# Where TensorE's expert products stand against its spreading products: two places of a gated-expert kernel moved

## The chip, the cores and the metric

The kernel runs on one core of one Trainium2 chip. The metric is the device time of one execution in microseconds (us). Five engines work side by side and meet at semaphores: TensorE (PE), VectorE (DVE), ScalarE (ACT), GpSimd (POOL) and SyncE (SP), which only issues DMAs. Each engine takes its own instructions strictly in the order in which the program lists them, so an instruction that waits holds up all that stand behind it on its engine.

## What is computed

The input is x, 16 images of 64 channels and 112 x 112 positions, in float32.

```python
def _L0_conv_ref(x, conv_w, conv_b):
    pooled = jnp.stack([jnp.max(x, axis=1), jnp.mean(x, axis=1)], axis=1)
    y = conv 3x3 (pooled, 2 channels -> 1) + conv_b
    return x * sigmoid(y)

def _L0_ffn_ref(x, router_w, router_b, expert_w, expert_b):   # E = 8 experts, K = 2
    router_probs = softmax(x @ router_w + router_b)
    top_p, top_i = top_k(router_probs, K);  top_p = top_p / sum(top_p)
    expert_out = einsum('bnd,edc->bnec', x, expert_w) + expert_b
    return einsum('bnk,bnkc->bnc', top_p, take(expert_out, top_i))

x = x + _L0_conv_ref(_ln_c(x), conv_w, conv_b)        # norm over channels
t = tokens(x)                                         # one token per position, 64 values
t = t + _L0_ffn_ref(_ln_t(t), router_w, router_b, expert_w, expert_b)
```

So each position gets a scale from a small convolution, a router picks two of eight 64 x 64 experts for it, and the output is the input plus the two gated expert products.

## The kernel before, in words

The 16 images are 8 pairs; a pair fills the 128 partitions. A pair is worked in 14 steps of 8 image rows (896 columns, `TOK`, two halves of 448, `HALF`). Three stages run on different pairs at the same time, one round behind the other:

- **Centring (A)**, rounds 0 to 7: PE multiplies a transposed slice of the input by the centring matrix and the router weights (`centre_rows`, L493), two groups per step; ACT copies the result out (L942, L946) and squares it, DVE takes maxima and sums (L687, L697).
- **Gates (B)**, rounds 1 to 8: on whole-pair statistics. DVE works at fixed places between its other work: an inverse square root, then the top-two router (`gate`: L729 to L835). POOL has router products as well (L1240 to L1311). In step 2 PE makes the small convolution (L592, `convolve`), ACT its sigmoid (L1026, "sig").
- **Experts (C)**, rounds 2 to 10: step `v` of the pair two rounds back. PE turns the gates (`turn`, L507), ACT brings them to SBUF (L991), PE spreads them over partitions into PSUM (`spread`, L514), DVE multiplies spread gates by the input (`scale_unit`, L710, units 0 to 5), for units of POOL ACT first copies the spread gates out of PSUM ("gs", `gate_to_sbuf`, L999) and POOL multiplies (L1201), and PE multiplies the eight products by the expert weights (`experts`, L568). PE also spreads the scale of the convolution (`spread_a1`, L553), ACT copies it ("a1s", L1006), POOL multiplies it with the input ("tt", L1218), and DVE adds both (`finish`, L723). SP loads and stores.

Rounds 2 to 7 have all three stages ("rounds with centring"). Round 8 has gates and experts, round 9 experts alone, and round 10 is a short rest ("rounds without centring").

The spread gates have two PSUM slots. Slot 0 takes DVE's units 1, 2, 4, 5; slot 1 takes DVE's units 0 and 3 and both units of POOL, whose copy by ACT must be done before the slot is written again. So a spreading product of unit 2, 4 or 5 waits for the DVE unit before it in the slot (`scaled_d`). The order on PE in one step, with the names that the texts use:

- S1, SP1: spreading for DVE's unit 1 and POOL's second unit; E5': expert product of unit 5 of the step before; T: the turn for the next step; bias and E0
- S2, S3: the second spreading batch; centring group 0; E1, EP0 (unit 1 and POOL's first)
- S4, SP0': the third batch, for unit 4 and POOL's first unit of the next step; in step 2 of a round the convolution; E2; A1 (`spread_a1`); bias and E3
- S5, S0': the fourth batch, unit 5 and unit 0 of the next step; centring group 1; E4, EP1

Every E is two products of 448 columns, which the trace shows as four records (float32 takes two each). The waits: E2 waits for DVE's unit 2, as S4 does; E5' waits for unit 5 of the step before, as S1 does. SP0' waits for unit 3, SP1 for unit 0. `centre_rows` of group 1 waits for ACT's a1s copy, since both use the PSUM tile tm. In step 2 A1 waits for the sigmoid, for the same reason. ACT's order is gs for POOL's first unit, (in step 2 the sigmoid), a1s, squares, copy of centring group 1, squares. POOL takes its unit as soon as gs is copied and DVE has passed a given place of the gates, and then the tt product. DVE's order in a step: early gates, unit 1, finish, units 2 and 3, (maximum of group 0), late gates, unit 4, finish, unit 5, unit 0 of the next step, (maximum of group 1).

Of the kernel before, what the change touches and what calls it, by code (L numbers as in the profile page):

```python
# [135 lines left out]
def gated_expert_program(nc, x, conv_w, conv_b, router_w, router_b, expert_w, expert_b, const_f, const_g, out):  # L136
# [3 lines left out]
    with ExitStack() as ctx:  # L140
# [132 lines left out]
        def due(count):  # L273

            return count > 0
# [10 lines left out]
        def c_at(r, per_step, v, n):  # L286
            return at(r, 2, per_step * STEPS, per_step * v + n)
# [4 lines left out]
        def on(r, v):  # L292

            return 0 <= (r - 2) * STEPS + v < PAIRS * STEPS
# [173 lines left out]
        def _(pe):  # L468
# [5 lines left out]
            def centre_rows(r, step, g):  # L474
                if g == 0:
                    if due(count := at(r, 0, STEPS // XA * 16, (step // XA + 1) * 16)):
                        pe.wait_ge(ld_xa[step % XA], count)
                read_out(pe, r, step, g + 1 - len(centre_pairs(r)))
                v = step - LAG
                if on(r, v + 1) and g == 0:  # L480
                    if due(count := c_at(r, 1, v + 1, 1)):
                        pe.wait_ge(s_ready, count)
                if on(r, v + 1) and g == 1:
                    if due(count := c_at(r, 1, v + 1, 1)):
                        pe.wait_ge(a1_out, count)
                if step == 2 and g == 1 and r >= 2:
                    b_done(pe, r, B_ACT, "sig")
                pair = centre_pair(r, step, g)
                for j in range(GRP):
                    row = g * GRP + j  # L490
                    for b in range(2):
                        chans = slice(b * CH, (b + 1) * CH)
                        last = pe.matmul(pair[:, b, j, :],  # L493
                                         xa[chans, step % XA, row * W:(row + 1) * W], rhs1[chans, :],
                                         start=True, stop=True)
                last.then_inc(centred, 1)

            def turn(r, step, v):

                if due(count := c_at(r, 1, v, 1)):  # L500
                    pe.wait_ge(rest1, count)
                read_out(pe, r, step, 0)
                if due(count := c_at(r, 1, v - 1, 1)):
                    pe.wait_ge(a1_out, count)
                for j in range(ROWS):
                    for b in range(2):
                        last = pe.transpose(turn_out[b * SB:(b + 1) * SB, j * W:(j + 1) * W],  # L507
                                            parts[:, v % 2, j, b * SB:(b + 1) * SB], ident)
                last.then_inc(turned, 1)

            def spread(v, k, c, slot):
                for b in range(2):
                    rows = slice(b * SB + slot * QUAD, b * SB + (slot + 1) * QUAD)
                    last = pe.matmul(gb[:, 2 * slot + b, 0:HALF], cg[rows, k * P:(k + 1) * P],  # L514
                                     s[rows, v % 2, c * HALF:(c + 1) * HALF], start=True, stop=True)
                return last

            def spread_for_dve(r, v, i):

                if i == 0:  # L520
                    if due(count := c_at(r, NP, v, 1)):
                        pe.wait_ge(gate_out, count)
                elif i == 3:
                    if due(count := c_at(r, NP, v, 2)):
                        pe.wait_ge(gate_out, count)
                else:
                    before = {1: 0, 2: 2, 4: 3, 5: 5}[i]
                    if due(count := c_at(r, ND, v, before)):
                        pe.wait_ge(scaled_d, count)
                spread(v, D_PAIR[i], i // 3, 1 if i in (0, 3) else 0).then_inc(spread_d, 1)  # L530

            def spread_for_pool(r, v, j):

                if j == 0:
                    if due(count := c_at(r, 1, v, 1)):
                        pe.wait_ge(s_ready, count)
                    if due(count := c_at(r, ND, v - 1, 4)):
                        pe.wait_ge(scaled_d, count)
                else:
                    if due(count := c_at(r, ND, v, 1)):  # L540
                        pe.wait_ge(scaled_d, count)
                spread(v, P_PAIR, j, 1).then_inc(spread_p, 1)
# [15 lines left out]
            def biases(r, v, c):  # L558
                if due(count := c_at(r, 2, v - 1, c + 1)):
                    pe.wait_ge(final, count)  # L560
                for b in range(2):
                    pe.matmul(moe[b * CH:(b + 1) * CH, c, 0:HALF], bw[:, b * CH:(b + 1) * CH],  # L562
                              s[:, v % 2, c * HALF:(c + 1) * HALF],
                              start=True, stop=False, skip_group_check=True)

            def experts(u, k, c):
                for b in range(2):
                    last = pe.matmul(moe[b * CH:(b + 1) * CH, c, 0:HALF], wc[:, k * CH:(k + 1) * CH],  # L568
                                     gx[:, u, b, :], start=False, stop=(k == KT - 1), skip_group_check=True)
                last.then_inc(mixed, 1)  # L570

            def experts_of_dve(r, v, i):
                if due(count := c_at(r, ND, v, i + 1)):
                    pe.wait_ge(scaled_d, count)
                experts(i, D_PAIR[i], i // 3)

            def experts_of_pool(r, v, j):
                if due(count := c_at(r, NP, v, j + 1)):
                    pe.wait_ge(scaled_p, count)
                experts(ND + j, P_PAIR, j)  # L580
# [29 lines left out]
            def body(r, A, Bp, steps=STEPS):  # L610
                for step in range(steps):
                    v = step - LAG
                    cur, ahead = on(r, v), on(r, v + 1)

                    if cur:
                        spread_for_dve(r, v, 1)
                        spread_for_pool(r, v, 1)
                    if on(r, v - 1):
                        experts_of_dve(r, v - 1, 5)
                    if ahead:  # L620
                        turn(r, step, v + 1)
                    if cur:
                        biases(r, v, 0)
                        experts_of_dve(r, v, 0)

                    if cur:
                        spread_for_dve(r, v, 2)
                        spread_for_dve(r, v, 3)
                    if A:
                        centre_rows(r, step, 0)  # L630
                    if cur:
                        experts_of_dve(r, v, 1)
                        experts_of_pool(r, v, 0)

                    if cur:
                        spread_for_dve(r, v, 4)
                    if ahead:
                        spread_for_pool(r, v + 1, 0)
                    if Bp and step == 2:
                        convolve(r, A)  # L640
                    if cur:
                        experts_of_dve(r, v, 2)
                    if ahead:
                        spread_a1(r, step, v + 1, A, Bp)
                    if cur:
                        biases(r, v, 1)
                        experts_of_dve(r, v, 3)

                    if cur:
                        spread_for_dve(r, v, 5)  # L650
                    if ahead:
                        spread_for_dve(r, v + 1, 0)
                    if A:
                        centre_rows(r, step, 1)
                    if cur:
                        experts_of_dve(r, v, 4)
                        experts_of_pool(r, v, 1)

            early_body(0, False)
            early_body(1, True)  # L660
            pe.wait_ge(setup_dve, 2)
            body(2, True, True)
            for r in range(3, PAIRS):
                body(r, True, True)
            body(PAIRS, False, True)
            body(PAIRS + 1, False, False)
            body(PAIRS + 2, False, False, LAG + 1)
# [736 lines left out]
```

## Time and profile before

| | us |
|---|---|
| median of 3 runs (1415.57 to 1417.33) | 1415.97 |
| profiled execution | 1416.11 |
| span of its instructions | 1414.3 |
| PE busy | 1308.1 (92%) |
| DVE busy | 1240.0 (88%) |
| POOL busy | 1066.4 (75%) |
| ACT busy | 1053.7 (75%) |

The span is what the timeline covers, from 0 to 1414.3; 1.8 us of the profiled execution lie around it. PE and DVE are both near full, so a share over the whole span does not say which of them sets the end; that changes from step to step and has to be read in the timeline. A row of a timeline gives the start, the length of the merged records, engine, line, operation, tiles and count, and in brackets the idle time before and what ended it. Ends overlap a little with the next start, so distances are taken from start to start.

### The profile page before, as it was taken

The numbers are of one execution on the slowest core, as the hardware profiler recorded it, in microseconds if no ns is written. First come the engines' busy times: TensorE is split into PE (matmuls) and PEld (weight loads), VectorE is DVE, ScalarE is ACT, GpSimd is POOL, SyncE is SP. The second block draws the span as 40 slices with busy tenths as digits, with TensorE's granted clock in tenths as the row PEclk, the third lists the DMA queues.
The fourth block names the chain that finished last, engine by engine and source line by source line (L and its number), as shares of the span: only waits on it lengthen the run. The fifth ranks groups of instructions, "written<-read, shape, count | busy, mean of one in ns | idle before, by whom it ended". The sixth has DMA issues, their size and how long they took to land.

```text
span 1414.3 us, 33104 instructions
## 1 busy us (share of the span) xinstructions
PE 1308.1 (92%) x11750; PEld 617.7 (44%) x11750; DVE 1240.0 (88%) x1527; ACT 1053.7 (75%) x3950; POOL 1066.4 (75%) x643
## 2 busy tenths in 40 slices
PE   8864999999999999999999999999999898899998
PEld 8853444444444444444444444444444332233332
DVE  6787799979999899988999899988999789987776
ACT  5677789888988898888988889888898344444442
POOL 6333687887788787887888787887878887887765
PEclk9955899999999999999999999999999999999999
DMA  6442466667667666576666666676665555565663
GB/s 224 131 128 66 144 196 199 202 188 210 202 188 218 189 208 209 173 233 196 197 184 209 197 199 205 176 224 196 202 210 165 155 164 156 159 183 180 178 188 118
DMA packets 85845, 259.97 MB, mean 184 GB/s; under 512 B 13744, under 2 KB 13744, under 8 KB 85680
## 3 DMA queue, kind: packets, MB, share of 16 engines
q1 hardware_dynamic: 85680, 257.85, 60.5%
q8 instruction: 94, 1.54, 0.5%
q14 instruction: 71, 0.58, 0.1%
HBM read 206.42 MB, written 51.38 MB: 182 GB/s over the span
## 4 chain that ended last, share of the span: by engine, by line
PE 52%; DVE 24%; issue 12%; POOL 2%; ACT 1%; DVEq 0%; POOLq 0%; ACTq 0%
PE moe L568 30%; DVE gx L710 15%; PE gb L514 8%; PE tm L493 8%; DVE ge L732 2%; PE tm L507 2%; DVE stats L687 2%; PE moe L562 2%; DVE ot L723 1%; PE tm L553 1%; DVE oh L745 1%; PE tm L592 1%; DVE u L795 1%; POOL dl L1261 1%; DVE top L729 0%
## 5 line engine op out<-in xcount | busy, mean ns | idle before, releaser
L568 PE MATMUL moe<-gx,wc 128*64 128x448 f32 x3584 | 812.6, 553 | 0.0
L710 DVE TENSOR_TENSOR gx<-gb,xd 128x896 f32<-128x896 f32 x672 | 707.5, 1085 | 84.9 <-PE gb L514 84.4
L1201 POOL TENSOR_TENSOR gx<-gs,xd 128x896 f32<-128x896 f32 x224 | 492.9, 2201 | 249.7 <-ACT gs L999 181.6
L999 ACT ACTIVATE gs<-gb 128x896 f32<-128x896 f32 x224 | 205.2, 916 | 190.1 <-PE gb L514 184.6
L961 ACT ACTIVATE sq<-xct 112x64 f32<-112x64 f32 x1400 | 338.4, 246 | 7.5 <-DVE early_s L697 2.1
L568 PEld LDWEIGHTS moe<-gx,wc 128*64 128x64 f32 x3584 | 218.0, 136 | 193.5 <-issue 160.8
L961 ACT ACTIVATION_READ_ACCUMULATOR sq<-xct 112x1 f32 x1400 | 265.5, 190 | 0.0
L514 PE MATMUL gb<-s,cg 32*128 32x448 f16 x1792 | 187.1, 359 | 61.4 <-DVE gx L710 60.3
L1218 POOL TENSOR_TENSOR tt<-xc,a1s 128x896 f32<-128x896 f32 x112 | 235.0, 2098 | 11.3 <-issue 9.7
L514 PEld LDWEIGHTS gb<-s,cg 32*128 32x128 f16 x1792 | 51.5, 91 | 399.8 <-DVE gx L710 333.7
L493 PE MATMUL tm<-rhs,xa 64*112 64x74 f32 x2800 | 185.5, 274 | 10.5 <-ACT early_l L946 5.2
L493 PEld LDWEIGHTS tm<-rhs,xa 64*112 64x112 f32 x2800 | 162.4, 183 | 45.3 <-issue 39.9
L723 DVE TENSOR_TENSOR ot<-moe,tt 128x448 f32<-128x448 f32 x224 | 137.9, 616 | 34.2 <-PE moe L568 34.2
L942 ACT ACTIVATE xct<-tm 112x512 f32<-112x512 f32 x175 | 103.9, 594 | 59.3 <-PE tm L493 59.2
L1006 ACT ACTIVATE a1s<-tm,ones 128x896 f32<-128x896 f32 x112 | 112.9, 1008 | 40.6 <-PE tm L553 40.6
L1207 POOL TENSOR_TENSOR parts<-q,parts 112x448 f16<-112x448 f32 x112 | 115.8, 1034 | 9.4 <-ACT parts L984 9.4
L991 ACT ACTIVATE s<-tm 128x896 f16<-128x896 f16 x112 | 101.6, 907 | 0.4 <-PE tm L507 0.4
L687 DVE TENSOR_REDUCE stats<-xct 112x8 f32<-112x512 f32 x128 | 86.7, 677 | 6.9 <-ACT logit_mean L946 6.6
L507 PEld LDWEIGHTS tm<-cg,parts 112*64 112x64 f16 x1792 | 60.0, 111 | 56.2 <-issue 56.2
L687 DVE TENSOR_REDUCE early_s<-xct 112x8 f32<-112x512 f32 x96 | 65.1, 678 | 19.2 <-ACT early_l L946 18.5
L562 PE MATMUL moe<-s,bw 128*64 128x448 f16 x448 | 81.0, 355 | 0.0
L984 ACT ACTIVATE parts<-q 112x576 f16<-112x576 f32 x112 | 76.0, 678 | 0.0
(94 smaller groups left out, 1089.8 us busy)
## 6 DMA issues: line engine op xcount, KB each, us to landing
xd<-in_x_dram SPq DMA_DIRECT2D x448, 224.0 KB, 4.0
xa<-in_x_dram SPq DMA_DIRECT2D x112, 448.0 KB, 4.3
xc<-in_x_dram SPq DMA_DIRECT2D x112, 448.0 KB, 4.7
out_dram<-ot SPq DMA_DIRECT2D x112, 448.0 KB, 3.5
gx<-in_const_g_dram SPq DMA_DIRECT2D x1, 384.0 KB, 5.4
cf<-in_const_f_dram SPq DMA_DIRECT2D x1, 333.5 KB, 2.9
cf<-in_L_ffn_expert_b_dram SPq DMA_DIRECT2D x12, 1.0 KB
gx<-in_L_ffn_expert_w_dram SPq DMA_DIRECT2D x1, 128.0 KB, 5.2
```

The lines of the kernel that those rows point to most:

```text
L493: last = pe.matmul(pair[:, b, j, :], xa[chans, step % XA, row * W:(row + 1) * W], rhs1[chans, :], start=True, stop=True)
L514: last = pe.matmul(gb[:, 2 * slot + b, 0:HALF], cg[rows, k * P:(k + 1) * P], s[rows, v % 2, c * HALF:(c + 1) * HALF], start=True, stop=True)
L568: last = pe.matmul(moe[b * CH:(b + 1) * CH, c, 0:HALF], wc[:, k * CH:(k + 1) * CH], gx[:, u, b, :], start=False, stop=(k == KT - 1), skip_ ...
L687: dve.tensor_reduce(to[:, 0, lo + cols.start:lo + cols.stop], xct[:, step % 2, cols, :], AX.X, ALU.max) \
L710: dve.tensor_tensor(gx[:, i, :, :], gb[:, 2 * slot:2 * slot + 2, 0:HALF], xd[:, v % 2, :, c * HALF:(c + 1) * HALF], ALU.mult).then_inc(sca ...
L723: dve.tensor_tensor(ot[:, sl, cols], moe[:, c, 0:HALF], tt[:, sl, cols], ALU.add).then_inc(final, 1)
L961: last = act.activation(sq[:, n, :], xct[:, step % 2, n, :], ACT.Square, accum_out=to[:, 1, lo + n:lo + n + 1])
L999: act.activation(gs[:, j, :, :], gb[:, 2:4, 0:HALF], ACT.Copy).then_inc(gate_out, 1)
L1006: act.activation(a1s[:, v % 2, :].rearrange("p (c t) -> p c t", c=2), tm[:, :, 0:HALF], ACT.Identity, bias=ones[:, :], scale=1.0).then_inc ...
L1201: pool.tensor_tensor(gx[:, ND + j, :, :], gs[:, j, :, :], xd[:, v % 2, :, j * HALF:(j + 1) * HALF], ALU.mult).then_inc(scaled_p, 1)
L1207: pool.tensor_tensor(quadrants(v)[:, :, :, QN:QUAD], q_blocks(v, AGAIN, BLOCK), high_again(v), ALU.subtract).then_inc(rest1, 1)
L1218: pool.tensor_tensor(tt[:, sl, :], xc[:, sl, :], a1s[:, sl, :], ALU.mult).then_inc(scaled_x, 1)
```

## The change

Two calls on PE move; no instruction is added or removed on any engine. `experts_of_dve(r, v, 2)` (E2) goes ahead of S4 and SP0' in all rounds, and so ahead of the convolution in step 2. `experts_of_dve(r, v - 1, 5)` (E5') goes ahead of S1 and SP1, but only in rounds without centring (`not A`).

```diff
                     cur, ahead = on(r, v), on(r, v + 1)
 
+                    if not A and on(r, v - 1):
+                        experts_of_dve(r, v - 1, 5)
                     if cur:
                         spread_for_dve(r, v, 1)
                         spread_for_pool(r, v, 1)
-                    if on(r, v - 1):
+                    if A and on(r, v - 1):
                         experts_of_dve(r, v - 1, 5)
                     if ahead:
                         turn(r, step, v + 1)
...
                     if cur:
+                        experts_of_dve(r, v, 2)
                         spread_for_dve(r, v, 4)
                     if ahead:
                         spread_for_pool(r, v + 1, 0)
                     if Bp and step == 2:
                         convolve(r, A)
-                    if cur:
-                        experts_of_dve(r, v, 2)
                     if ahead:
                         spread_a1(r, step, v + 1, A, Bp)
```

On PE, step 2 of a round with centring, before. The row L592 is the convolution, L553 is A1, L514 are spreading batches and L568 expert products (here x2 is one E):

```order
 L568 MATMUL moe<-gx,wc 64x448 x4
 L514 MATMUL gb<-s,cg 128x448 x4
 L592 MATMUL tm<-pooled,band 112x224 x6
 L568 MATMUL moe<-gx,wc 64x448 x2
 L553 MATMUL tm<-s,cg 64x448 x4
 L562 MATMUL moe<-s,bw 64x448 x2
 L568 MATMUL moe<-gx,wc 64x448 x2
 L514 MATMUL gb<-s,cg 128x448 x4
 L493 MATMUL tm<-rhs,xa 112x74 x8
```

and the same place now:

```order
 L568 MATMUL moe<-gx,wc 64x448 x6
 L514 MATMUL gb<-s,cg 128x448 x4
 L592 MATMUL tm<-pooled,band 112x224 x6
 L553 MATMUL tm<-s,cg 64x448 x4
 L562 MATMUL moe<-s,bw 64x448 x2
 L568 MATMUL moe<-gx,wc 64x448 x2
 L514 MATMUL gb<-s,cg 128x448 x4
 L493 MATMUL tm<-rhs,xa 112x74 x8
```

E2 joins E1 and EP0 ahead of S4 and SP0', and A1 follows the convolution directly. In the other steps with centring the row L592 is missing and all else is the same.

On PE, one step of a round without centring, before, from E1 and EP0 on (S4 and SP0', E2, A1, bias, E3, S5 and S0', E4 and EP1, S1 and SP1, E5', T):

```order
 L568 MATMUL moe<-gx,wc 64x448 x4
 L514 MATMUL gb<-s,cg 128x448 x4
 L568 MATMUL moe<-gx,wc 64x448 x2
 L553 MATMUL tm<-s,cg 64x448 x4
 L562 MATMUL moe<-s,bw 64x448 x2
 L568 MATMUL moe<-gx,wc 64x448 x2
 L514 MATMUL gb<-s,cg 128x448 x4
 L568 MATMUL moe<-gx,wc 64x448 x4
 L514 MATMUL gb<-s,cg 128x448 x4
 L568 MATMUL moe<-gx,wc 64x448 x2
 L507 MATMUL tm<-cg,parts 64x112 x16
```

and now:

```order
 L568 MATMUL moe<-gx,wc 64x448 x6
 L514 MATMUL gb<-s,cg 128x448 x4
 L553 MATMUL tm<-s,cg 64x448 x4
 L562 MATMUL moe<-s,bw 64x448 x2
 L568 MATMUL moe<-gx,wc 64x448 x2
 L514 MATMUL gb<-s,cg 128x448 x4
 L568 MATMUL moe<-gx,wc 64x448 x6
 L514 MATMUL gb<-s,cg 128x448 x4
 L507 MATMUL tm<-cg,parts 64x112 x16
```

Both single expert products have joined the pairs before them, and S4/SP0' and S1/SP1 come one expert product later.

## Rows read from the trace of the kernel before

**Rows 1.** Rounds 5, 8, 9: stretch, length, busy PE, PEld, DVE, ACT, POOL, clock.

```profile
606.13:767.75 161.62, 155.84 (x1470) 71.56 (x1468) 149.22 (x185) 141.25 (x588) 129.87 (x73) 1.00 0.66 200
1090.98:1249.18 158.20, 138.99 (x1022) 49.82 (x1020) 143.47 (x157) 65.29 (x90) 127.43 (x73) 1.00 0.56 163
1249.18:1392.56 143.38, 135.60 (x1011) 47.80 (x1009) 103.91 (x112) 59.43 (x72) 108.04 (x59) 1.00 0.62 180
```

**Rows 2.** Waits of DVE in round 9: total us, times, longest.

```profile
DVE gx L710 <- PE gb L514: 26.4, 28, 1.0
DVE ot L723 <- PE moe L568: 13.1, 28, 0.6
```

**Rows 3.** Timeline of PE, a step of round 9.

```profile
1334.50 0.36 PE L514 MATMUL gb<-s,cg 32*128 32x448 f16 x2
1335.19 0.36 PE L514 MATMUL gb<-s,cg 32*128 32x448 f16 x2 [0.32 <-DVE gx L710]
...
1336.29 0.55 PE L553 MATMUL tm<-s,cg 128*64 128x448 f16 x4
...
1337.71 0.37 PE L514 MATMUL gb<-s,cg 32*128 32x448 f16 x4
1338.01 1.72 PE L568 MATMUL moe<-gx,wc 128*64 128x448 f32 x8
1339.66 0.36 PE L514 MATMUL gb<-s,cg 32*128 32x448 f16 x2
1340.26 0.36 PE L514 MATMUL gb<-s,cg 32*128 32x448 f16 x2 [0.23 <-DVE gx L710]
...
1341.35 0.56 PE L507 MATMUL tm<-cg,parts 112*64 112x112 f16 x16
```

**Rows 4.** Timeline of PE, the last expert products of the program.

```profile
1408.22 2.48 PE L568 MATMUL moe<-gx,wc 128*64 128x448 f32 x12
```

**Rows 5.** Timeline of PE, step 8 of round 5 and the next.

```profile
704.19 0.37 PE L514 MATMUL gb<-s,cg 32*128 32x448 f16 x4
...
705.29 0.55 PE L553 MATMUL tm<-s,cg 128*64 128x448 f16 x4
...
706.71 0.37 PE L514 MATMUL gb<-s,cg 32*128 32x448 f16 x4
707.03 1.01 PE L493 MATMUL tm<-rhs,xa 64*112 64x74 f32 x16
...
712.55 0.37 PE L514 MATMUL gb<-s,cg 32*128 32x448 f16 x4 [0.31 <-DVE gx L710]
```

**Rows 6.** Timeline of ACT in that step.

```profile
704.64 0.92 ACT L999 ACTIVATE gs<-gb 128x896 f32<-128x896 f32 x1
705.88 1.01 ACT L1006 ACTIVATE a1s<-tm,ones 128x896 f32<-128x896 f32 x1 [0.33 <-PE tm L553]
```

**Rows 7.** Timeline of PE, step 2 of round 5.

```profile
634.44 2.52 PE L592 MATMUL tm<-pooled,band 112*112 112x224 f32 x12
...
637.70 0.55 PE L553 MATMUL tm<-s,cg 128*64 128x448 f16 x4
```

**Rows 8.** Timeline of ACT in that step.

```profile
637.00 0.47 ACT L1026 ACTIVATE sig<-tm,cb 112x224 f32<-112x224 f32 x1 [1.50 <-PE tm L592]
```

**Rows 9.** Timeline of POOL, step 8 of round 5.

```profile
705.69 2.15 POOL L1201 TENSOR_TENSOR gx<-gs,xd 128x896 f32<-128x896 f32 x1 [2.40 <-ACT gs L999]
707.79 2.10 POOL L1218 TENSOR_TENSOR tt<-xc,a1s 128x896 f32<-128x896 f32 x1
```

**Rows 10.** Timeline of DVE, late gate of step 8 and early gate of step 9.

```profile
704.26 1.08 DVE L732 TENSOR_TENSOR ge<-dl,top 112x896 bf16<-112x896 f32 x1
...
709.72 0.66 DVE L737 TENSOR_TENSOR key<-ge,prio 112x896 bf16<-112x896 bf16 x1
```

**Rows 11.** Timeline of POOL, step 10 of round 8.

```profile
1206.95 1.74 POOL L1261 TENSOR_TENSOR dl<-oh,g 112x896 f32<-112x896 bf16 x1
```

**Rows 12.** Timeline of DVE in that step.

```profile
1207.36 2.28 DVE L732 TENSOR_TENSOR ge<-lg,top 112x896 bf16<-112x896 f32 x1
```

## The prediction

> **What bounds the kernel now.** I read the busy time of three stretches first, each from one T of step 0 to the T that ends the round: round 5 as a round with centring, then rounds 8 and 9 [rows 1]. The granted clock is 1.00 in all three (2.4 GHz), so no term comes from the clock. A round with centring takes 161.62 us, and PE is busy for 155.84 of it: PE bounds it, with DVE (149.22) close behind. Round 9 takes 143.38 us, 10.24 a step; PE is busy for 135.60, DVE for only 103.91, and the waits of DVE in it say for whom it stands: 26.4 us for spreading products and 13.1 for expert products [rows 2]. So there PE's own list is the bound. Round 8 lies between: 158.20 us with PE at 138.99 and DVE at 143.47; there the bound changes from half step to half step.
>
> Then I read the timelines. In round 9, S4 starts at 1334.50 but SP0' only at 1335.19, after an idle time that DVE's unit 3 ends; S1 at 1339.66 and SP1 at 1340.26, ended by unit 0 [rows 3]. Behind each stalled product stands an expert product that could run. In the steps with centring the same batches run as one (x4) without a stall [rows 5]: centring has given DVE time. That is what decides the two halves of the sum.
>
> **The change, rounds 9 and 10.** An expert product ahead of another costs 0.76 us: 12 records take 2.48 [rows 4], 8 take 1.72 [rows 3]. A full batch takes about 0.34 up to its successor in this list (0.30 where an expert product follows). Third batch: S4 to A1 took 1336.29 - 1334.50 = 1.79; now E2 and the batch together take 0.76 + 0.34 = 1.10, a gain of 0.69. First batch: S1 to T took 1341.35 - 1339.66 = 1.69; now also 1.10, a gain of 0.59. What comes next for PE? S4 now starts 0.76 later, unit 4 starts 0.41 after it and takes 1.09, S5 needs its end: S4 + 1.5. PE itself reaches S5 at S4 + 0.34 + (1337.71 - 1336.29) = S4 + 1.76. Unit 1 against S2 is the same sum. ACT's gs copy starts 0.45 after a batch and takes 0.92 [rows 6], so S0' (S4 + 1.37) is in time too. Unit 3 and unit 0 are done 0.2 before SP0' and SP1 are reached. DVE stays at 7.4 us of work in a step of 8.95, POOL at 7.7, so nothing takes the place of the stalls. The first kind falls away 16 times (steps of round 9 and two of round 10), the second 15 times: 16 x 0.59 + 15 x 0.69 = **-19.8 us**.
>
> **Rounds with centring: nothing to gain, three things to lose.** PE's list is only reordered; S4 and SP0' come 0.76 later, A1 where it was.
>
> First, ACT. It copies gs 0.45 after S4 starts and a1s behind it, and in its order gs is first. Before, a1s started 1.69 after S4 (705.88 - 704.19), having waited 0.33 for A1 [rows 5, 6]. Now it starts at 0.76 + 0.45 + 0.81 = 2.02, the 0.81 being what one gs copy takes up to the next instruction: 0.33 later. Centring group 1 waits for that copy. It started 1.15 after a1s did, and 0.32 after S5 where it starts 0.30 after S5 when free [rows 5, 6]: the copy is already what releases it, by a hair. So it goes 0.33 to 0.34 later. Of the 14 steps of a round, four have this distance (5, 8, 9, 13), three have 0.1 to 0.25 more (3, 4, 10; 12 as 10), the others far more since S5 waits for DVE's late gates. Where the next S2 waits for DVE the loss is taken up (after 8, 10, 12). Left: 3 x 0.34 (5, 9, 13) + 0.23 (3) + 0.10 (4) = 1.35. In step 6 ACT also joins two buffers between a1s and its copy of group 1, which DVE takes up without a pause; its delay of about 0.30 passes to the next S2.
>
> Second, the convolution. It runs from 634.44, ACT's sigmoid from 637.00 for 0.47, and A1, at 637.70, needs it [rows 7, 8]. E2 stood between and covered the sigmoid. Now the convolution and the sigmoid are 0.76 later, the sigmoid reaches PE some 0.13 after its end: A1 at 637.60 + 0.76 = 638.36, 0.66 late. E2's work has gone ahead of it but S4's place is as much later, so this is lost: 0.66 a round.
>
> Third, POOL against DVE. POOL's unit starts when gs is copied (705.69, idle 2.40 before it), and the tt product ends at 707.79 + 2.10 = 709.89. DVE's key product, started at 709.72, ends 0.49 after that [rows 9, 10]. A product ge takes 1.08 with POOL idle [rows 10] but 2.28 when POOL is at work, ending 0.95 after POOL's instruction, 1206.95 + 1.74 [rows 11, 12]. So such a gate product waits for POOL's running instruction to end. Move POOL by 0.76, and the key product of step 9 ends 0.76 later; S2 of step 9 already waits for DVE (0.31) [rows 5], so it is 0.76 late. The key product of step 13 starts just as tt ends: 0.51 late by the same sum; that of step 11 too, but there a later gate product waits for POOL anyway and gives all but 0.08 back. 0.76 + 0.51 + 0.08 = 1.35.
>
> The Trainium skill, "SBUF — State Buffer", section "Who interferes with whom", says that GpSimd and a VectorE instruction with two SBUF inputs exclude each other for the whole instruction; the trace agrees, with ge at 2.28 against 1.08. By the opposite view, a shared bandwidth, the shift would cost nothing here and the total below would be 8 us less.
>
> A round with centring: 1.35 + 0.30 + 0.66 + 1.35 = 3.66. Five whole ones (3 to 7) and round 2, which begins with other waits, at some 3.2: **+21.5 us**. The bounds: only the convolution's term is certain to be felt (6 x 0.66 = 4); if every delay of 0.33 were felt in all 84 steps on top of the gates' terms, 28 + 8 + 4 = 40. I take 21.5, since each term is tied to one row.
>
> **Round 8.** By PE alone it would win as round 9, 14 x 1.28 = 18. But PE has 19 us of idle time, and over half of it ends with a gate. POOL's second unit starts with SP1's copy, which now comes 0.21 later after S5 than before (0.76 + 0.45 against 0.59 + 0.41), and the router products behind it hold up ge and its like [rows 11, 12]: in five places (steps 3, 5/6, 10, 12, and 0 with 0.76) a later gate is what the next batch waits for. Half steps without such a product win 0.58 (step 2), 0.23 (4) and 0.11 (8). 0.76 + 4 x 0.21 - 0.92 = **+0.7 us**. Bounds: -9 (locks never decide, half the gain of PE) and +4.
>
> **Sum.** 1416.11 (span 1414.3 and 1.8 around it) - 19.8 + 21.5 + 0.7 = 1418.5; the profiled execution is 0.14 above the median, so 1418.4. I say **1418**.
>
> **Rivals.**
> - *The reordering is absorbed.* POOL and DVE do not collide as I say, since all move together. Then the gates' 1.35 falls from six rounds (-8), and round 8 wins 5 instead of losing 0.7: 1418.4 - 8 - 6 = 1404; if only one of the two, about 1411. For it: DVE is not full in any round, and POOL sits idle before most units [rows 9]. Against it: lengths of ge and key follow POOL's ends to 0.02 us.
> - *ACT becomes the bound with centring (the other side).* ACT has 141.25 of 161.62 us busy [rows 1]. The place is centring group 1 behind a1s; if the 0.33 is felt in each step without a long stall at S5 (10 of 14) and not taken up by S2's stalls, a round loses 10 x 0.33 + 0.66 + 1.35 = 5.3, six 32: 1416 - 20 + 32 = 1428. It decides as soon as more than about 3.3 us a round are lost, which outweighs round 9's gain. For it: the wait of 0.33 before a1s is ACT's slack there and is used up.
> - *The gain in round 9 stays out.* Units 1 and 4 start 0.76 later, and DVE, not PE, would set the step; DVE's chain in half a step is 3.6 us against PE's 4.5, so this needs what no row shows. If half the gain goes: 1428.
>
> **How the numbers follow.** My forecast 0.50, own range 1413 to 1424; absorbed 0.25 (1403 to 1412); ACT 0.20 (1424 to 1432); gain stays out 0.05. The range that leaves out two in ten: 1408 to 1427. A measurement tells 0.2%, 2.8 us, from no change: faster below 1413.1, slower above 1418.8. Faster takes the absorbed case and little of mine: 0.27. Mine straddles the upper edge: same 0.35, slower 0.38.
>
> **What would show it.** Round 9 at 8.95 us a step, S4/SP0' and S1/SP1 as x4 without idle time. In rounds with centring: 165.3 us a round; centring group 1 at 3.17 after the old place of S4; a PE stall of 0.66 at A1 in step 2, with the sigmoid as releaser; the key products of steps 9, 11 and 13 at 1.0 to 1.4 us where they took 0.61 to 0.66. Round 8 near 158.9. A round with centring below 163 us, or round 9 above 9.4 us a step, would prove the sum wrong.

## The result, and the profile after

The changed kernel takes 1421.45 us (median of 6 runs, 1419.05 to 1422.95) against 1415.76 for the kernel before (6 runs): the ratio is 1.0042, 95% interval 1.0032 to 1.0053. It is slower, by more than the 0.2% that can be told from no change. The profiled execution took 1421.24, its span is 1419.4.

The first view is again the busy time by stretch, from T to T: round 5, round 8, round 9, and then two short pieces of round 8 (start and end in us, length, busy PE, PEld, DVE, ACT, POOL with counts, granted clock, DMA share, GB/s).

```profile
615.44:780.63 165.19, 155.97 (x1471) 71.54 (x1469) 151.10 (x185) 140.09 (x588) 127.86 (x73) 1.00 0.64 196
1110.96:1273.81 162.85, 134.90 (x1024) 48.01 (x1020) 147.45 (x156) 63.91 (x89) 128.61 (x73) 0.96 0.55 157
1273.81:1398.56 124.75, 124.75 (x1014) 44.41 (x1010) 103.88 (x112) 57.87 (x71) 106.99 (x60) 1.00 0.72 207
1119.50:1124.40 4.90, 4.73 (x22) 1.33 (x24) 4.01 (x6) 0.00 (x0) 3.37 (x2) 0.65 0.38 99
1189.00:1193.60 4.60, 4.34 (x20) 1.31 (x20) 4.45 (x6) 0.00 (x0) 3.45 (x2) 0.66 0.27 73
```

Against [rows 1], a round with centring is 3.57 us longer (165.19 against 161.62), round 8 is 4.65 longer (162.85 against 158.20), and round 9 is 18.63 shorter (124.75 against 143.38). PE is busy all through round 9: it has no idle time left. The granted clock of round 8 has dropped to 0.96; the last two rows say where, and [rows 1] had 1.00 there.

The span by stages, from the starts of the T that bound them: 0.88 later at the first T of the program, 1.26 in the rest of round 2, 17.84 in rounds 3 to 7, 4.65 in round 8, -18.63 in round 9, -0.90 in the rest; together +5.1, as the spans say (1419.4 - 1414.3). The first two of these are no measure of the change. The program is the same up to the first T, and in the fourteen profiles of this case that T starts anywhere between 130.39 and 132.51. Round 2 begins at the low level of TensorE's clock (in the kernel before the granted clock is 0.50 from 110 to 149 us and 1.00 from 149.3 to 160), and where the clock comes back differs from profile to profile, whatever the order. In the kernel before it was still low for these expert products (first row); in e1, an experiment below with the old order up to round 8, it was not (second row):

```profile
146.10 3.25 PE L568 MATMUL moe<-gx,wc 128*64 128x448 f32 x8
146.67 1.72 PE L568 MATMUL moe<-gx,wc 128*64 128x448 f32 x8
```

With the old order round 2, from its first T, takes 152.50 to 152.68 us in three profiles and 150.09 to 150.19 in four. The profile of the changed kernel had the clock back early (153.76), that of the kernel before late (152.50). Like with like, round 2 is about 3.6 us longer (153.76 against 150.19), not 1.26.

Round 9, the timeline of PE in one step:

```profile
1355.76 2.48 PE L568 MATMUL moe<-gx,wc 128*64 128x448 f32 x12
1358.17 0.37 PE L514 MATMUL gb<-s,cg 32*128 32x448 f16 x4
1358.47 0.57 PE L553 MATMUL tm<-s,cg 128*64 128x448 f16 x4
...
1362.62 0.37 PE L514 MATMUL gb<-s,cg 32*128 32x448 f16 x4
1362.91 0.58 PE L507 MATMUL tm<-cg,parts 112*64 112x112 f16 x16
```

The batches that stood apart as two x2 in [rows 3] are one x4 each, without idle time, and the next instruction starts 0.30 behind. The waits of DVE in round 9 answer to [rows 2]:

```profile
DVE gx L711 <- PE gb L514: 17.3, 28, 0.6
```

DVE now waits 17.3 us for spreading products, and the view lists no wait for expert products any more: DVE gets its additions in time. It still waits, so PE is still the bound.

Step 8 of round 5, PE and then ACT, against [rows 5, 6]:

```profile
715.87 0.37 PE L514 MATMUL gb<-s,cg 32*128 32x448 f16 x4
716.17 0.57 PE L553 MATMUL tm<-s,cg 128*64 128x448 f16 x4
...
717.62 0.37 PE L514 MATMUL gb<-s,cg 32*128 32x448 f16 x4
718.28 1.01 PE L493 MATMUL tm<-rhs,xa 64*112 64x74 f32 x16 [0.29 <-ACT a1s L1007]
```

```profile
716.32 0.92 ACT L1000 ACTIVATE gs<-gb 128x896 f32<-128x896 f32 x1 [0.84 <-PE gb L514]
717.13 1.00 ACT L1007 ACTIVATE a1s<-tm,ones 128x896 f32<-128x896 f32 x1
```

ACT now waits for SP0', then runs gs and a1s without a pause (before, it waited for A1 between them), and PE stands 0.29 before centring group 1. S4's old place is 715.87 - 0.76 = 715.11; centring starts 3.17 after it, exactly the sum of the prediction. In the same step, POOL and then DVE, against [rows 9, 10]:

```profile
719.47 2.10 POOL L1219 TENSOR_TENSOR tt<-xc,a1s 128x896 f32<-128x896 f32 x1
```

```profile
720.68 1.36 DVE L738 TENSOR_TENSOR key<-ge,prio 112x896 bf16<-112x896 bf16 x1
```

The key product took 0.66 before. It ends at 722.04, 0.47 after tt does (721.57). The other two that the prediction names take 1.14 (step 11, 0.62 before) and 1.11 (step 13, 0.61 before). And step 2, PE and ACT, against [rows 7, 8]:

```profile
644.50 2.52 PE L592 MATMUL tm<-pooled,band 112*112 112x224 f32 x12
647.66 0.57 PE L553 MATMUL tm<-s,cg 128*64 128x448 f16 x4 [0.64 <-ACT sig L1027]
```

```profile
647.06 0.46 ACT L1027 ACTIVATE sig<-tm,cb 112x224 f32<-112x224 f32 x1 [1.50 <-PE tm L592]
```

A1 has a stall of 0.64 with the sigmoid as releaser.

What the prediction did not have is in round 8, step 6. POOL, DVE and PE there (the first row of DVE is the kernel before, the second the changed kernel):

```profile
1182.44 2.14 POOL L1202 TENSOR_TENSOR gx<-gs,xd 128x896 f32<-128x896 f32 x1
1184.53 1.03 POOL L1208 TENSOR_TENSOR parts<-q,parts 112x448 f16<-112x448 f32 x1
1185.51 1.74 POOL L1241 TENSOR_TENSOR lg<-logit_mean,rho 112x896 f32<-112x896 f32 x1
```

```profile
1161.50 3.10 DVE L732 TENSOR_TENSOR ge<-lg,top 112x896 bf16<-112x896 f32 x1
1183.02 5.19 DVE L733 TENSOR_TENSOR ge<-lg,top 112x896 bf16<-112x896 f32 x1
```

```profile
1189.26 0.56 PE L514 MATMUL gb<-s,cg 32*128 32x448 f16 x4 [4.14 <-DVE gx L711]
1189.75 3.64 PE L568 MATMUL moe<-gx,wc 128*64 128x448 f32 x12
```

The gate product ge, 1.08 when alone, takes 5.19: it started while POOL's gx product ran, and ended 0.96 after the third of three POOL instructions that followed each other without a gap (1185.51 + 1.74 = 1187.25). The kernel before had a milder form of this, which the prediction overlooked: there ge started while POOL's parts product ran, waited for it and for the lg product behind it, and took 3.10. In the changed kernel PE stands 4.14 us for the unit behind ge. Then its next 12 records take 3.64 us instead of the 2.48 of round 9, in the stretch where the granted clock is 0.66, which is a mean over time spent at each of the two levels, 1.2 and 2.4 GHz. Steps 0, 1 and 7 have the same pair, a stall of 2.3 to 2.8 us and then 12 records in 4.17, 3.62 and 3.90: together (4.17 + 3.62 + 3.64 + 3.90) - 4 x 2.48 = 5.4 us. Not every stall of that size does it: step 11 has two, of 2.80 and 2.35, and the 12 records behind each took 2.48.

### The profile page after: what moved, and what is told of

It reads as the page before. It is cut to its first block, busy times and chain, and to the rows that moved or that the text cites. A ratio compares the mean times of both kernels' runs of the same rounds, so it can differ in the third digit from the quotient of the medians.

```text
span 1419.4 us, 33104 instructions
## 1 busy us (share of the span) xinstructions
PE 1291.3 (91%) x11750; PEld 611.7 (43%) x11750; DVE 1255.4 (88%) x1527; ACT 1044.0 (74%) x3950; POOL 1055.2 (74%) x643
## 4 chain that ended last, share of the span: by engine, by line
PE 47%; DVE 25%; issue 13%; ACT 5%; POOL 2%; DVEq 0%; ACTq 0%; POOLq 0%
PE moe L568 28%; DVE gx L711 13%; PE tm L493 7%; PE gb L514 6%; DVE stats L688 2%; ACT a1s L1007 2%; DVE ot L724 2%; DVE key L738 2%; PE tm L507 2%; DVE ge L733 1%; PE tm L592 1%; PE moe L562 1%; PE tm L553 1%; DVE oh L746 1%; ACT sq L962 1%
## 5 line engine op out<-in xcount | busy, mean ns | idle before, releaser
L568 PE MATMUL moe<-gx,wc 128*64 128x448 f32 x3584 | 784.3, 551 | 0.0
L1202 POOL TENSOR_TENSOR gx<-gs,xd 128x896 f32<-128x896 f32 x224 | 480.4, 2145 | 265.7 <-ACT gs L1000 221.3
L568 PEld LDWEIGHTS moe<-gx,wc 128*64 128x64 f32 x3584 | 230.4, 137 | 233.8 <-issue 170.4
L514 PE MATMUL gb<-s,cg 32*128 32x448 f16 x1792 | 166.6, 360 | 69.9 <-DVE gx L711 68.3
L514 PEld LDWEIGHTS gb<-s,cg 32*128 32x128 f16 x1792 | 45.3, 91 | 394.5 <-DVE gx L711 313.8
```

The source lines that it names most:

```text
L1202: pool.tensor_tensor(gx[:, ND + j, :, :], gs[:, j, :, :], xd[:, v % 2, :, j * HALF:(j + 1) * HALF], ALU.mult).then_inc(scaled_p, 1)
```

## Experiments: which rounds

All edits are against the changed kernel, except that of e7, which is against the kernel before. The kernel before was timed beside each group of four, and every ratio is to those runs. The cuts show the new conditions; where such a condition is false, the call stands at its old place. Lengths of rounds come from one profiled execution of each kernel, totals are medians.

**e1, rounds 9 and 10 alone.**

```diff
-                    if not A and on(r, v - 1):
+                    if r > PAIRS and on(r, v - 1):
                         experts_of_dve(r, v - 1, 5)
...
-                    if cur:
+                    if cur and r > PAIRS:
                         experts_of_dve(r, v, 2)
```

> The changed order only in rounds 9 and 10; rounds 2 to 8 in the order of before. Theory (the sum by stages): rounds 2 to 8 as before (161.6 us a round with centring, 158.2 for round 8), round 9 at 124.8 us instead of 143.4, the rest 0.9 shorter: 1416 - 19.5 = 1396.5. Rival (round 9 is only that short because the rounds ahead of it end later and its loads are further along): round 9 above 130 us, 1402 or more.

Measured: 1395.0 us, ratio 0.9856 (0.9841 to 0.9871). The first row is round 8, the second round 9:

```profile
1089.80:1247.00 157.20, 138.49 (x1022) 49.60 (x1018) 141.88 (x156) 64.75 (x89) 127.81 (x73) 1.00 0.57 163
1247.00:1371.74 124.74, 124.74 (x1012) 44.41 (x1008) 103.94 (x112) 57.92 (x71) 106.91 (x60) 1.00 0.72 207
```

The theory holds: rounds 9 and 10 give their 19.5 us alone (124.74 for 143.38, and 0.88 in the rest). The total is 21 us below the 1416.27 of the runs beside it, more than the 19.5, because this profile also had a shorter round 2 (150.19 for 152.50, the clock told of above) and a shorter round 8 (157.20 for 158.20), both in the old order.

**e2, all rounds without centring** (e1 with `not A` in place of `r > PAIRS`).

> The changed order in all rounds without centring (8 to 10); rounds 2 to 7 as before. Theory: rounds 2 to 7 lose nothing, round 8 keeps its 162.9 us (158.2 before) with its slow stretches of TensorE, round 9 124.8: 1396.5 + 4.7 = 1401. Rival (round 8 is longer only because round 7 hands it a later start of ScalarE and GpSimd): round 8 at 158.9 or less, 1397.

Measured: 1400.24 us, ratio 0.9896 (0.9879 to 0.9912). Round 8:

```profile
1090.25:1251.82 161.57, 134.77 (x1024) 47.61 (x1020) 146.94 (x156) 64.03 (x89) 128.46 (x73) 0.96 0.56 159
```

Round 8 is long although rounds 2 to 7 are as before, so its loss is its own. The clock is 0.96 again.

## Experiments: the loss in rounds with centring

**e3, SP0' ahead of E2 in rounds with centring.**

```diff
+                    if A and ahead:
+                        spread_for_pool(r, v + 1, 0)
                     if cur:
                         experts_of_dve(r, v, 2)
                         spread_for_dve(r, v, 4)
-                    if ahead:
+                    if not A and ahead:
                         spread_for_pool(r, v + 1, 0)
```

> The changed kernel, but in rounds with centring SP0' stays ahead of E2 and only S4 goes behind it. Theory (ScalarE's gs copy and with it a1s and GpSimd were made late by SP0', not by S4): a round with centring falls from 165.2 to about 162.3 us, which is before plus the 0.65 at A1 in step 2; the stalls before centring group 1 go away, the key products are back at 0.61 to 0.66 us; total 1421 - 17 = 1404. Rival 1 (what costs is that S4 and unit 4 are late): no change, 165 us a round. Rival 2 (the joined expert products themselves cost PE time): 164 to 165 us a round.

Measured: 1424.33 us, ratio 1.0061 (1.0046 to 1.0076), 165.55 us a round. The number is none of the three expected. PE in step 8 of round 5:

```profile
719.02 0.36 PE L514 MATMUL gb<-s,cg 32*128 32x448 f16 x2
719.31 0.97 PE L568 MATMUL moe<-gx,wc 128*64 128x448 f32 x4
720.22 0.36 PE L514 MATMUL gb<-s,cg 32*128 32x448 f16 x2
720.51 0.57 PE L553 MATMUL tm<-s,cg 128*64 128x448 f16 x4
...
721.95 0.37 PE L514 MATMUL gb<-s,cg 32*128 32x448 f16 x4
722.27 1.01 PE L493 MATMUL tm<-rhs,xa 64*112 64x74 f32 x16
```

```profile
724.95 0.62 DVE L740 TENSOR_TENSOR key<-ge,prio 112x896 bf16<-112x896 bf16 x1
```

The stall before centring group 1 is gone and the key product is back at 0.62, as the theory wants. But the edit added a cost of its own: two products (x2) take PE 0.29 to the next start, and four (x4) take 0.30. Split, the batch costs twice. SP0' to A1 is 720.51 - 719.02 = 1.49, where E2 and a joined batch took 1.10 before (705.29 - 704.19 in [rows 5]): 0.29 more is the second half of the batch, and the rest is E2, which takes 0.91 to the next start between the two halves and took 0.80 before. Step 8 went from 10.92 in the kernel before to 11.33. The length of the round is closest to Rival 1 (no change, 165 us), for a reason that no theory had. So e3 confirms the two signs, but its total could not tell the theories apart. The next four runs take one suspected cost at a time instead.

**e5, E2 behind the convolution again.**

```diff
-                    if cur:
+                    if cur and not (A and step == 2):
                         experts_of_dve(r, v, 2)
...
                         convolve(r, A)
+                    if cur and A and step == 2:
+                        experts_of_dve(r, v, 2)
```

> The changed kernel, but in step 2 of rounds with centring E2 stands behind the convolution again. Theory (E2 covered ScalarE's sigmoid): the stall of 0.64 before A1 goes away, a round with centring falls from 165.2 to about 164.55 us, six rounds 3.9 us: 1417.5. Rival (the stall only moves on, to S5 or centring group 1 of the same step): step 2 stays at 14.0 us and the total at 1421.

Measured: 1414.26 us, ratio 0.9997 (0.9987 to 1.0006). A round:

```profile
614.59:779.02 164.43, 155.96 (x1470) 71.42 (x1468) 151.11 (x185) 140.18 (x588) 127.35 (x73) 1.00 0.65 197
```

0.76 less than 165.19, a little more than the 0.64 expected, and step 2 is down from 14.03 to 13.36: the theory holds. The total fell by more than 6 x 0.76 = 4.6. In the profile round 8 took 157.94, in the same order as the 162.85 of the changed kernel; how that can be is told under round 8 below.

**e6 and e7, a short tt product, in the changed kernel and in the one before.**

```diff
-                pool.tensor_tensor(tt[:, sl, :], xc[:, sl, :], a1s[:, sl, :], ALU.mult).then_inc(scaled_x, 1)
+                n = 64 if r < PAIRS and v in (7, 11) else TOK
+                pool.tensor_tensor(tt[:, sl, 0:n], xc[:, sl, 0:n], a1s[:, sl, 0:n], ALU.mult).then_inc(scaled_x, 1)
```

> The changed kernel; in rounds 2 to 7 GpSimd's tt product of steps 8 and 12 takes only 64 of 896 columns (the rest of that output is left out). Theory (VectorE's key product of the step after waits for the running tt product): the key products of steps 9 and 13 fall from 1.36 to about 0.62 us, S2 of those steps comes about 0.5 earlier, a round falls from 165.2 to about 164.1 us: 1415. Rival (the key product is long for another reason, or S2 waits for ScalarE as well): key products or round length unchanged, 1421.

> The kernel before with the same two tt products of rounds 2 to 7 cut to 64 columns (that part of the output left out), as a control. Theory: the tt product was out of the way there, so the key product of step 9 falls by 0.04 only and a round stays within 0.1 us of 161.6: 1416. Rival (less work on GpSimd shortens any round): about 1 us a round less, 1410.

Measured: e6 1413.27 us, ratio 0.9984 (0.9971 to 0.9998); e7 1414.29 us, ratio 0.9993 (0.9984 to 1.0003). A round of e6, and one of e7:

```profile
614.06:777.97 163.91, 156.00 (x1470) 71.51 (x1468) 150.15 (x185) 139.96 (x588) 124.05 (x73) 1.00 0.65 197
```

```profile
604.68:766.18 161.50, 155.83 (x1471) 71.44 (x1469) 149.14 (x185) 141.31 (x588) 125.94 (x73) 1.00 0.66 200
```

The same work taken from POOL is worth 1.28 us a round in the changed kernel and 0.12 before. So it is not POOL's load but where its product stands. The key product of step 9 in e6:

```profile
719.31 0.61 DVE L738 TENSOR_TENSOR key<-ge,prio 112x896 bf16<-112x896 bf16 x1
```

**e8, a short a1s copy.**

```diff
+                n = 32 if 2 < r < PAIRS else HALF
-                act.activation(a1s[:, v % 2, :].rearrange("p (c t) -> p c t", c=2), tm[:, :, 0:HALF], ACT.Identity,
+                act.activation(a1s[:, v % 2, :].rearrange("p (c t) -> p c t", c=2)[:, :, 0:n], tm[:, :, 0:n],
```

> The changed kernel; in rounds 3 to 7 ScalarE's a1s copy takes 32 of 448 columns of each half (the rest left out), so it ends some 0.7 us sooner while all starts ahead of it stay. Theory (centring group 1 waits for a1s, which is late behind gs): the stalls of 0.15 to 0.30 before centring group 1 go away in steps 3, 5, 8, 9, 13, and the copy behind the join in step 6 comes earlier: a round falls by 0.16 + 3 x 0.30 + 0.3 = 1.4 to 163.8 us, total 1414. Rival (those stalls cost nothing, VectorE sets these steps): 165 us a round, 1421.

Measured: 1412.2 us, ratio 0.9976 (0.9962 to 0.9990). A round, and PE in step 8:

```profile
614.23:777.73 163.50, 155.42 (x1470) 71.24 (x1468) 150.83 (x185) 130.94 (x588) 127.37 (x73) 1.00 0.65 197
```

```profile
715.58 0.37 PE L514 MATMUL gb<-s,cg 32*128 32x448 f16 x4
715.88 1.01 PE L493 MATMUL tm<-rhs,xa 64*112 64x74 f32 x16
```

The stall is gone and a round is 1.69 shorter. More than the 1.4 expected: step 7 also became 0.5 shorter, behind the join of step 6. A short copy wins a little by itself, though. Step 8 now takes 10.87, less than the 10.92 of the kernel before, where the same copy released centring group 1 by 0.02 us. No run has the short a1s copy in the kernel before, as e7 has the short tt product.

**e9, the three together** (the edits of e5, e6 and e8).

> The changed kernel with three edits at once: E2 behind the convolution in step 2, the short tt product (steps 8 and 12, rounds 2 to 7) and the short a1s copy (rounds 3 to 7); parts of tt and a1s are left out. Theory (the whole loss of 3.6 us in a round with centring is these three): 165.2 - 0.75 - 1.27 - 1.7 = 161.5 us a round, as before the change (161.6). Rival (part of the loss is something else, or the terms overlap): 162.3 us or more.

Measured: 1401.55 us, ratio 0.9894 (0.9878 to 0.9911). A round:

```profile
607.51:769.06 161.55, 155.46 (x1473) 71.20 (x1471) 149.88 (x185) 131.08 (x588) 123.87 (x73) 1.00 0.66 200
```

161.55, as before the change: the three terms (0.76 + 1.28 + 1.69 = 3.73) hold the 3.57. Their sum is larger because the shortened instructions give a little that the change never took (0.12 by e7 for tt, an unknown small part for a1s); that the three places hold nearly all of the loss is shown, the last tenth or two are not. The total is near that of e2 (1400.24), since round 8 took 162.76 in this profile: its loss is there whatever the rounds before it do.

## Experiments: round 8

**e4, products that fill the stalls.** The operands are constants and the result goes to columns that nobody reads.

```diff
+            def fill(r, v, n):
+                pe.wait_ge(a1_out, c_at(r, 1, v + 1, 1))
+                for _ in range(n):
+                    pe.matmul(tm[:, 1, HALF:512], cg[:, 0:P], cg[:, 0:512 - HALF], start=True, stop=True)
...
+                    if r == PAIRS and step in (0, 1, 6, 7):
+                        fill(r, v, 72 if step == 6 else 36)
                     if cur:
                         spread_for_dve(r, v, 5)
```

> The changed kernel with 36 small extra products (64 columns, float16, result not used) on PE in the long stalls before S5 of round 8, steps 0, 1 and 7, and 72 in step 6, each group behind ScalarE's a1s copy. Theory (the stalls of 2.3 to 4.1 us are followed by a granted clock of 0.65, at which 12 records of expert products take 3.6 to 4.2 us instead of 2.48): with PE busy there the clock stays at 1.00 and round 8 falls from 162.9 to about 157.5 us, total 1416. Rival (these products are slow because their operands come late from VectorE or GpSimd): round 8 unchanged or longer, 1421 or more.

Measured: 1418.02 us, ratio 1.0017 (1.0007 to 1.0026), against 1.0042. PE in step 6 of round 8:

```profile
1184.62 2.27 PE L585 MATMUL tm<-cg 128*128 128x64 f16 x72 [0.51 <-ACT a1s L1014]
1188.27 0.37 PE L514 MATMUL gb<-s,cg 32*128 32x448 f16 x4 [1.37 <-DVE gx L718]
1188.57 2.48 PE L568 MATMUL moe<-gx,wc 128*64 128x448 f32 x12
```

S5 still waits for the unit behind ge (5.20 us there too), but the 12 records behind it are back at 2.48. All four filled places are. Round 8 took 158.96: less was won than the 5.4, because one more slow group (3.84) came up in step 9, where nothing was filled. The rival, late operands, falls: the operands came as late as before, and the products are fast.

How firm this is differs by place, since slow groups come and go between profiles of this same order of round 8. Seven profiles have it unfilled (the changed kernel, e2, e3, e5, e6, e8, e9). The group behind the stall of step 1 is slow in all seven, and that of step 6 in all six that have the stall; for these two places the theory is shown. Those of steps 0 and 7 are slow in three and in four of the seven, so that they were fast in e4 proves little. The first group of step 11 is slow in four of them.

**e10, e11, e12, parts of the change in round 8**, all with rounds 2 to 7 as before and rounds 9 and 10 as changed: E5' alone; E2 alone; both, in steps 2, 4 and 8 only (conditions as in e1, with `r == PAIRS` and the steps added).

> Rounds 2 to 7 as before, rounds 9 and 10 as changed, and in round 8 only E5' ahead of S1 and SP1. Theory (a stall above about 2 us is followed by slow products; GpSimd's copy for its second unit starts 0.2 later behind E5', and stalls grow where a gate follows router products): round 8 at 159 to 161 us (157.2 to 158.2 in the old order), total 1397 to 1399, slow products in steps 0 or 1. Rival (E5' alone is harmless, E2 does the damage in round 8): 157 us, 1395 or less.

> Rounds 2 to 7 as before, rounds 9 and 10 as changed, and in round 8 only E2 ahead of S4 and SP0'. Theory (E2's move wins 0.69 in half steps without a gate, but in step 6 VectorE comes early to a gate product and then waits for a run of GpSimd products): round 8 at 156 to 160 us, total 1394 to 1398, no slow products in steps 0 and 1. Rival (E2 does the damage alone): 161.5 us or more as with both moves, 1400.

> A try at a better kernel: rounds 2 to 7 as before, rounds 9 and 10 as changed, and in round 8 both moves only in steps 2, 4 and 8, where PE and not a gate sets the pace. Theory: 0.6 in step 2, 0.2 in step 4, 0.1 in step 8: round 8 about 1 us below 157.2, total 1394. Rival (any earlier start hands VectorE's gate product of step 6 to a run of GpSimd products): round 8 at 158 or more, 1396 to 1397.

| | total us | ratio (interval) | round 8 us | ge of step 6 us |
|---|---|---|---|---|
| e1, neither | 1395.0 | 0.9856 (0.9841 to 0.9871) | 157.2 | 1.38 |
| e10, E5' | 1394.2 | 0.9847 (0.9833 to 0.9862) | 156.1 | 1.75 |
| e11, E2 | 1396.5 | 0.9863 (0.9848 to 0.9877) | 158.1 | 3.78 |
| e12, steps 2, 4, 8 | 1393.5 | 0.9843 (0.9829 to 0.9858) | 156.4 | 3.10 |
| e2, both | 1400.2 | 0.9896 (0.9879 to 0.9912) | 161.6 | 5.15 |

E5' alone missed my expectation of 159 to 161: it is harmless. Its stalls of 2.02, 2.06 and 2.42 us were followed by no slow group. E2 alone came inside its range, 156 to 160, with two slow groups (8 records in 2.60 and 2.41 us for 1.72, in steps 6 and 11). e12 came out as its theory said. Both moves together cost 5.2 us of total against e1, and here the four runs of e2 (1399.25 to 1402.75) lie above all those of e1 (1394.44 to 1397.40).

Why both, and not one? In each of the fourteen profiles ge starts 3.85 to 3.95 us after the T of step 6. What the moves shift is POOL. Its gx product of that place starts 1.18 us after the same T in the kernel before, 1.87 with E2 moved, 2.62 with E5' moved and 3.3 to 3.4 with both. Where ge waits to the end of POOL's run, it ends some 0.95 after the run does, so it takes 3.10, 3.78 and 5.2. But it does not always wait so long. The same place in e10, DVE and POOL:

```profile
1161.27 1.75 DVE L736 TENSOR_TENSOR ge<-lg,top 112x896 bf16<-112x896 f32 x1
```

```profile
1159.94 2.12 POOL L1205 TENSOR_TENSOR gx<-gs,xd 128x896 f32<-128x896 f32 x1
1162.03 1.88 POOL L1211 TENSOR_TENSOR parts<-q,parts 112x448 f16<-112x448 f32 x1
```

Here ge got its turn between two POOL instructions (it ended 0.96 after gx) and POOL's parts product took 1.88 instead of 1.03. It ended at 1163.02, before the parts product ended (1163.91) and before the lg product began, so it needs a result of neither. In e1 and e5 ge got its turn too. In e5, which has both moves, it started 0.61 after POOL's gx and took 2.46:

```profile
1178.58 2.46 DVE L736 TENSOR_TENSOR ge<-lg,top 112x896 bf16<-112x896 f32 x1
```

In e2 it started 0.62 after and in e6 0.60 after, and both lost, for 5.15 and 5.14 us. What decides who goes next is open.

So the lengths of round 8 in the table are not all of a kind. Where ge got its turn, the round took 157.2 (neither move), 156.1 (E5') and 157.9 (both, e5). Where it did not: 158.2 and 158.0 (neither, the kernel before and e7), 158.1 (E2) and 161.5 to 163.6 (both). Most of the loss of both moves, then, is the long wait of ge, and slow groups. Single runs spread by the same two things: those of e8 reach from 1407.70, with a mean granted clock of 0.973, to 1416.47, with 0.965. How much of it is the clock and how much is ge, no run separates. e12 is the best median, but its interval covers e1 and e10: four of the variants between 1393.5 and 1396.5 are not told apart by their intervals.

## Why the prediction came out as it did

It said 1418, with slower as the likeliest of three; measured were 1421.45. The direction and most terms came out by the mechanisms that it gave. The miss of 3 us is that of round 8. Step by step:

- **Rounds 9 and 10, -19.8:** measured -19.5 (-18.63 and -0.90), and e1 shows it alone. A step of round 9 takes 8.91 us against 8.95. PE stayed the bound, and the rival that the gain stays out is gone.
- **Rounds with centring, 3.66 a round:** measured 3.57. The stall at A1 was 0.64 for 0.66 (e5: 0.76 in all). The a1s stalls were 0.30 instead of 0.34 (3.17 after the old S4, as said); e8 puts them and the join at 1.69 against 1.35 + 0.30. The gates' terms of steps 9 and 13 were 0.76 + 0.51 = 1.27, and e6, which shortens just these two tt products, gives 1.28, of which 0.12 is not the change's (e7). Step 11 gave its delay back (12.19 against 12.18). The rivals "absorbed" and "ACT in each step" fell with that. Round 2 showed 1.26 for some 3.2, but by luck of the two profiles: like with like it is about 3.6. Rounds 2 to 7 are then 17.84 + 3.6 = 21.4 against 21.5.
- **Round 8, +0.7:** measured +4.65. This is the term that failed, by two steps of the prediction. One is "no term comes from the clock": the longer stalls of PE (2.3 to 4.1 us, where round 8 of the kernel before had none above 1.64) can be followed by products at the low clock, 5.4 us together in this profile. e4 shows that for steps 1 and 6. The other is "such a gate product waits for POOL's running instruction to end": it can wait for two or three that follow each other, 5.19 us in step 6. The trace of the kernel before had that already, with ge at 3.10 in the same place. Without the slow products the round would have taken about 157.4 (162.85 - 5.4), less than before.

The bound of "-9 and +4" for round 8 was too narrow by 0.65 on that side in this profile. The total stayed inside the range of 1413 to 1424, since the other terms were nearly right.

## What to carry to other kernels

An operation that is ready may go ahead of a stalled one, but only in the stages where the stall exists: here the same moves won 19.5 us where PE waited, and the one of E2 lost about 21 in rounds 2 to 7, where it did not. Before moving an issue point, follow the other engines' in-order lists from it (here SP0', gs, a1s, centring, and gs, POOL's unit, tt, the key product), since a wait that seems free by 0.02 us passes on all of the next delay. Before taking a difference of one stage from two profiles, look whether a second profile of the same order gives the same length: here round 2 moved by 2.3 us and round 8 by up to 5.6 without any edit to them. When an experiment moves instructions, look whether it splits a pair that runs for the price of one, as e3 did.

## What the runs showed of the hardware

- In round 8 of the changed kernel, after four of the six longest stalls of PE (2.28 to 4.14 us) the granted clock of the next 5 us is 0.64 to 0.66: 12 records take 3.62 to 4.17 us for 2.48. After the other two (2.80 and 2.35, step 11) it stays 1.00. Between profiles the length does not decide either: a stall of 1.95 in e2 was followed by slow records (3.94), and those of 2.02 to 2.42 in e10 were not. Small extra products in the stall kept the records at 2.48 (e4; firm for steps 1 and 6). The longest stall in round 8 of the kernel before was 1.64 us, and its granted clock was 1.00.
- Two spreading products take PE 0.29 us to the next start (e3), and four, the other two on other rows of the array, 0.30 (round 9 of the changed kernel).
- A DVE product with two SBUF inputs waits for POOL's running instruction, and may wait for those that follow it without a gap: 3.10 us for a product of 1.08 behind two (the kernel before), 5.19 behind three (step 6 of round 8, changed kernel). In other profiles of the same place it gets in between and ends 0.95 us after the first; POOL's next then takes 1.88 for 1.03 (e10).
